# Eight slots for the gathered x1 rows, and drains instead of semaphores between an engine's own steps in the scatters' stage

## The reference

```python
# layer 0, 8 heads of 16: attention of every edge within the edges of one dst
Q = (x[src] @ Wq + bq);  K = (x[dst] @ Wk + bk);  V = (x[dst] @ Wv + bv)
scores = einsum('ehd,ehd->eh', Q, K) / 4 + edge_attr @ Wb + bb
alpha = segment_softmax(scores, dst)
x1 = layernorm(x + segment_sum(alpha * V, dst) @ Wo + bo)
# layer 1: one softmax over all edges
h = x1 @ W;  e = leaky_relu((h @ a1)[src] + (h @ a2)[dst])
out = layernorm(x1 + segment_sum(softmax(e)[:, None] * h[src], dst))
```

## Time and profile before

| | us |
|---|---|
| median of 3 runs (lowest, highest) | 1265.93 (1257.95, 1266.73) |
| the profiled execution, its own time | 1259.13 |
| its span, first to last instruction | 1257.4 |
| around the span | 1.7 |
| granted TensorE clock, mean over the span | 0.782 of 2.4 GHz |
| PE, DVE, ACT, POOL busy | 718.7, 759.0, 717.2, 764.1 |
| first gather of x to the last | 4.7 to 593 |
| first gather of x1 to the last | 639.5 to 937.8 |
| first scatter to the last | 954.6 to 1255.7 |

### The profile page before, as it was taken

One profiled execution on the slowest core, in us unless ns is written; L12 is line 12 of the kernel. 1 busy time (PEld: TensorE's weight loads), 2 busy tenths in 40 slices (PEclk: granted clock), 3 DMA queues, 4 the chain that ended last, 5 costly groups with the idle time before them and its releaser, 6 DMA issues.

```text
span 1257.4 us, 14313 instructions
## 1 busy us (share of the span) xinstructions
PE 718.7 (57%) x3271; PEld 482.5 (38%) x3271; DVE 759.0 (60%) x3537; ACT 717.2 (57%) x2048; POOL 764.1 (61%) x807
## 2 busy tenths in 40 slices
PE   0357767767667767676844564546455554544441
PEld 0235445445445544444634454545442211111110
DVE  4487767767777668677756555546437444444442
ACT  3457777777777777777713343424347554444443
POOL 7665666666666666665056665666654666666666
PEclk9888888787887888878967777767767766777775
DMA  7365565566665656654155767667755333433331
GB/s 211 110 187 158 184 209 168 178 188 214 203 200 200 203 161 193 197 166 163 68 171 162 216 207 221 198 211 223 208 172 163 121 113 115 119 116 120 107 107 46
DMA packets 89104, 209.87 MB, mean 167 GB/s; under 512 B 20602, under 2 KB 22793, under 8 KB 89008
## 3 DMA queue, kind: packets, MB, share of 16 engines
q1 hardware_dynamic: 63802, 161.20, 40.4%
q0 software_dynamic: 25216, 47.76, 13.6%
HBM read 122.85 MB, written 90.07 MB: 169 GB/s over the span
## 4 chain that ended last, share of the span: by engine, by line
another core or an unknown queue 19%; DVE 17%; ACT 13%; issue 8%; PE 5%; POOL 1%; DMA 1%; DVEq 0%; SPq 0%; POOLq 0%
ACT yb L801 3%; ACT node_out L801 2%; ACT src_b L952 2%; PE psum L748 2%; DVE src_b L1477 2%; DVE match L1152 2%; ACT xsT L961 2%; DVE nst L1492 1%; DVE nst L1254 1%; POOL out_dram L524 1%; DMA x1d_in<-x_all 1%; DVE shift L1485 1%; ACT h_res L965 1%; DVE node_in L1247 1%
## 5 line engine op out<-in xcount | busy, mean ns | idle before, releaser
L518 POOL DMA_INDIRECT xs<-in_x,src_tab x196 | 185.7, 947 | 153.0 <-remote 74.6
L524 POOL DMA_INDIRECT out_dram<-yb,at_last x196 | 194.7, 993 | 120.7 <-ACT yb L801 64.6
L518 POOL DMA_INDIRECT xs<-x_all,row_tab x196 | 187.5, 957 | 114.9 <-issue 55.8
L518 POOL DMA_INDIRECT h_res<-in_x,dst_tab x196 | 188.9, 964 | 59.8 <-issue 59.8
L801 ACT ACTIVATE h_res<-node_in,shift,rstd 128x128 f32<-128x128 f32 (+1 forms) x392 | 155.8, 482 | 0.3 <-DVE shift L1284 0.3
L776 PE MATMUL psum<-src_b,ident_inv 128*128 128x512 f32 x90 | 69.6, 865 | 132.8 <-DVE src_b L1477 111.7
L961 ACT ACTIVATE xsT<-psum 128x512 f32<-128x512 f32 x48 | 28.7, 597 | 200.0 <-remote 165.8
L606 PE MATMUL psum<-h_res 128*128 128x512 f32 x98 | 68.7, 789 | 120.9 <-ACT h_res L808 120.0
L748 PE MATMUL psum<-w,xsT 128*128 128x129 f32 x384 | 80.7, 376 | 91.8 <-ACT xsT L961 80.4
L748 PEld LDWEIGHTS psum<-w,xsT 128*128 128x128 f32 x384 | 71.6, 278 | 99.1 <-ACT xsT L961 86.6
L610 PE MATMUL psum<-xsT,h_res 128*128 128x512 f32 x98 | 85.2, 966 | 32.2 <-ACT xsT L812 19.4
(11 more groups left out here) (312 smaller groups left out, 1915.5 us busy)
## 6 DMA issues: line engine op xcount, KB each, us to landing
x1d_in<-x_all SPq DMA_DIRECT2D x98, 256.0 KB
node_in<-in_x SPq DMA_DIRECT2D x48, 512.0 KB
x_all<-h_res SPq DMA_DIRECT2D x48, 512.0 KB
out_dram<-node_out SPq DMA_DIRECT2D x48, 512.0 KB
x_all<-yb SPq DMA_DIRECT2D x49, 256.0 KB
src_b<-src_t SPq DMA_DIRECT2D x49, 256.0 KB
agg_rows<-src_b SPq DMA_DIRECT2D x49, 256.0 KB
node_in<-x_all SPq DMA_DIRECT2D x24, 512.0 KB
```

The source lines that it names most:

```text
L518: return pool.indirect_dma_start(out=to, out_offset=None, in_=table, in_offset=bass.IndirectOffsetOnAxis(ap=idx, axis=0))
L524: return pool.indirect_dma_start(out=table, out_offset=bass.IndirectOffsetOnAxis(ap=idx, axis=0), in_=rows, in_offset=None, bounds_check=l ...
```

## The change

Four things. (1) In the second stage the gathered rows have eight slots: the four of `xs`, and the four of `yb`, whose stored rows of the first stage are out by then. POOL's wait is for `x1_T` of g-8. (2) The semaphores that count landings are one for the first two tiles of a group and one for the last two, in both gather stages; who waits, waits for both. `xd`, with eight slots, has them per slot modulo 4. (3) Waits are added: POOL (before the first gather of x1) and SP (before it loads the late node chunks) wait until the last three node chunks are stored, and ACT, before each half of a late chunk, until it is loaded. (4) In the third stage DVE and ACT have a drain where they waited for a semaphore of their own; `r_chain` and `xa_done` count groups, from group 1 on; `e_stats` and `e_log` are gone. And DVE's order is another: the moments of group s-1 stand between the running sums of group s.

```diff
+    XG = XS + YB
+    PAIR = G // 2
...
+        def x1_rows(g):
+            u = g % XG
+            return xs[:, u, :] if u < XS else yb[:, u - XS, :]
+        def x1_landed(g):
+            u = g % XG
+            halves = (src_head, src_rest) if u < XS else (dst_head, dst_rest)
+            in_first_stage = len(range(u % XS, GROUPS, XS))
+            return [half[u % XS] for half in halves], 16 * PAIR * (in_first_stage + use(g, XG))
+        def nodes_landed(eng):
+            for k in range(GROUPS - NX, GROUPS):
+                eng.wait_ge(x1_stored[k % NX], landed(k, NX))
...
                 if s == GROUPS:
-                    for u in range(NX):
-                        pass
+                    nodes_landed(sp)
...
-            for u in range(NX):
-                pass
+            nodes_landed(pool)
...
-                wait(pool, x1_T, g - XS + 1)
+                wait(pool, x1_T, g - XG + 1)
                 for t, idx in enumerate(columns(row_tab, g)):
-                    gather(tile(xs[:, g % XS, :], t), x1_all, idx)\
-                        .then_inc(last_x1 if g == END and t == G - 1 else got_x1[g % XS], 16)
+                    gather(tile(x1_rows(g), t), x1_all, idx)\
+                        .then_inc(last_x1 if g == END and t == G - 1 else x1_landed(g)[0][t // PAIR], 16)
...
-                    pe.wait_ge(got_x1[s % XS], use(s, XS) * 16 * G)
+                    wait_x1(pe, s)
...
+                        act.wait_ge(late_loaded[j % NI], use(j, NI) * 16)
...
-                fn(logs[:, 0:G], nmv[:, s % 2, :, 1], ACT.Ln, bias=eps_cols[:, 0:1]).then_inc(e_log, 1)
-                act.wait_ge(e_log, s)
+                fn(logs[:, 0:G], nmv[:, s % 2, :, 1], ACT.Ln, bias=eps_cols[:, 0:1])
+                act.drain()
...
             def running(g, t):
-                dve.wait_ge(xa_done, g * G + (t if g == 0 else G - 1) + 1)
-                wait(dve, r_chain, g * G + t)
+                if g == 0:
+                    dve.wait_ge(xa_done, t + 1)
+                    wait(dve, r_chain, t)
+                else:
+                    if t == 0:
+                        dve.wait_ge(xa_done, summed(g))
+                    dve.drain()
...
             def aggregates(b):
-                dve.wait_ge(e_stats, b)
                 if b == 2:
                     dve.wait_ge(first_shift_done, G)
-                wait(dve, e_shift, b - 2)
                 wait(dve, e_rstd, b - 2)
+                dve.drain()
...
                 if edge(s):
-                    for t in range(1, G):
-                        running(s, t)
+                    running(s, 1)
                 if edge(s - 1):
-                    moments(s - 1)
+                    dve.wait_ge(e_y, s - 1)
+                    moments(s - 1, 0)
+                    if edge(s):
+                        running(s, 2)
+                    moments(s - 1, 1)
+                    if edge(s):
+                        running(s, 3)
+                    moments(s - 1, 2)
+                    moments(s - 1, 3)
                     aggregates(s - 1)
```

More of the change, by code:

```diff
@@ L291, in gnn_kernel @@
         agg_stored, part_got = sems("agg_stored", NA), sem("part_got")
-        e_y, e_stats, e_var, e_log, e_rstd, e_shift, e_applied = (
-            sem("e_y"), sem("e_stats"), sem("e_var"), sem("e_log"), sem("e_rstd"), sem("e_shift"), sem("e_applied"))
+        e_y, e_var, e_rstd, e_shift, e_applied = sem("e_y"), sem("e_var"), sem("e_rstd"), sem("e_shift"), sem("e_applied")
         e_scat = sems("e_scat", YB)
@@ L315, in last_bank, with wait_pairs, wait_x1 @@
             return 3 if t < G // 2 else 5
+        def x1_rows(g):
[6 more added lines that the diff above has]
+            return [half[u % XS] for half in halves], 16 * PAIR * (in_first_stage + use(g, XG))
+        def wait_pairs(eng, halves, g):
+            for half in halves:
+                eng.wait_ge(half[g % XS], 16 * PAIR * use(g, XS))
+        def wait_x1(eng, g):
+            halves, value = x1_landed(g)
+            for half in halves:
+                eng.wait_ge(half, value)
         def use(k, ring):
@@ L535, in _ @@
                 for t, idx in enumerate(columns(src_tab, g)):
-                    gather(tile(xs[:, g % XS, :], t), x, idx).then_inc(got_src[g % XS], 16)
+                    gather(tile(xs[:, g % XS, :], t), x, idx).then_inc((src_head if t < PAIR else src_rest)[g % XS], 16)
                 if g == 0:
@@ L539, in _ @@
                 for t, idx in enumerate(columns(dst_tab, g)):
-                    gather(tile(xd[:, g % XD, :], t), x, idx).then_inc(got_dst[g % XD], 16)
+                    gather(tile(xd[:, g % XD, :], t), x, idx).then_inc((dst_head if t < PAIR else dst_rest)[g % XS], 16)
             pool.wait_ge(fix_dve, 1)
@@ L778, in _ @@
                     for t in range(G):
[L779 removed]
+                        last = tr(bank[7][:, t * P:(t + 1) * P], tile(x1_rows(END), t), ident[:, :])
                     last
@@ L948, in weigh @@
             def weigh(g, tiles=range(G)):
-                wait(act, r_chain, (g - 1) * G)
+                if g >= 2:
+                    act.wait_ge(r_chain, summed(g - 2))
                 for t in tiles:
                     i = g * G + t
-                    fn(tile(xa[:, g % 2, :], t), h_res[:, i * DH:i * DH + D], ACT.Copy, scale=att[:, i:i + 1])\
-                        .then_inc(xa_done, 1)
+                    last = fn(tile(xa[:, g % 2, :], t), h_res[:, i * DH:i * DH + D], ACT.Copy, scale=att[:, i:i + 1])
+                    if g == 0:
+                        last.then_inc(xa_done, 1)
+                if g > 0 and tiles.stop == G:
+                    last.then_inc(xa_done, 1)
             for u in range(NO):
@@ L1503, in aggregates, with shift_of @@
                 last.then_inc(e_var, 1)
+            def shift_of(b):
+                dve.wait_ge(e_rstd, b)
+                if b == 2:
+                    dve.wait_ge(first_applied, G)
+                wait(dve, e_applied, b - 2)
+                v.scalar_tensor_tensor(shift[:, b % 2, 0:G], nmv[:, b % 2, :, 0], -1.0, rstd[:, b % 2, 0:G],
+                                       ALU.mult, ALU.mult).then_inc(e_shift, 1)
             def first_rows(t):
@@ L1528, in _ @@
                 i = END * G + t
-                last = v.tensor_tensor_reduce(out=dots[:, t * D:(t + 1) * D], in0=tile(xs[:, END % XS, :], t),
+                last = v.tensor_tensor_reduce(out=dots[:, t * D:(t + 1) * D], in0=tile(x1_rows(END), t),
                                               in1=v_src[:, :], scale=1.0, scalar=0.0, op0=ALU.mult, op1=ALU.add,
@@ L1573, in _ @@
             running(2, 1)
-            moments(1)
+            dve.wait_ge(e_y, 1)
+            for t in range(G):
+                moments(1, t)
             aggregates(1)
```

42 lines of the change are left out of this document (19 added, 23 removed).

## The result

| | before | after |
|---|---|---|
| median, same chip | 1263.51 us (1257.95 to 1266.73, 4 runs) | 1290.67 us (1288.16 to 1292.32, 4 runs) |
| ratio, 95% interval | | 1.0233 (1.0191 to 1.0274) |
| profiled span | 1257.4 | 1288.6 |
| first gather of x1 | 639.5 | 642.7 |
| gathers of x1, first to last end | 298.3 | 315.8 |

The change makes the kernel 2.3% slower, where 1231 us and a gain were forecast. The 31 us of the span are 3.2 ahead of the gathers of x1, 17.5 in their stage, 6.3 between the stages, 4.0 in the scatters' stage, and none behind it. More than half of the loss is in the stage where the forecast said "no change", and in the stage in which it said "-30" it is slower too.

The account below looks back on a forecast made before the run. It took POOL's row of indirect DMAs (gathers 298 us, scatters 301 us) as the bound; 1259.1 - 39.4 (drains) + 9 (order) + 0 (eight slots) + 3 (small waits) = 1231.7, stated as 1231 us, chance 0.38, range 1180 to 1290.

Parts of the forecast that it names:

- -30: Scatters' stage: the forecast gain, from -39.4 us for the drains and +9 us for DVE's new order.
- Who makes POOL pause: Last two stages: not the gathers' landing, but semaphores seen late while POOL issues indirect DMAs; pauses 52 and 48 us.
- Eight slots, "I take 0": x1 gathers' stage: a lead of two more groups is used up once, then POOL waits as before; 0 us.
- The +33 us: x1 gathers' stage: upper bound if POOL sleeps for `row_done` and wakes 1.5 us later in each of 22 pauses.
- rival 3: x1 gathers' stage: POOL's pause ended by `row_done`, slower, 1295 us; sign a stage over 320 us; chance 0.22.
- Drains, -39.4: Third stage: DVE's late look at its own semaphore goes, POOL's ten pauses shrink to 0.3 us; -39.4 us.
- rival 2: Third stage: the hold only moves on, ACT still idle 10 us a cycle before `logs`; 1262 us; chance 0.23.
- The order, +9: Third stage: two running sums behind `e_y` reach PE about 0.9 us later in each of 10 cycles; +9 us.
- Small waits, +3: Pairs' landing semaphores and waits for stored and loaded chunks: +2 us, set at +3 with SP's wait.

Follow-up runs that it names:

- pause_long: Kernel before with 24 small memsets on POOL behind each group of x1 gathers and of scatters: 1.0046 of the kernel before.
- pool_drain: Kernel before with a drain of POOL behind each group of four DMAs in the last two stages: 1.1567 of the kernel before.
- slots_alone: Changed kernel with eight slots and POOL's wait for g-8, but the third stage of the kernel before: 1.0177 of the kernel before.
- before_lead4: Kernel before (four slots) with LEAD 4 instead of 6: 1.0169 of the kernel before.
- before_again: Kernel before, unchanged, measured again under another name: 0.9974 of the kernel before.
- four_ahead_drains_old_order: Changed kernel, but POOL waits for the transposition of four groups before and all four running sums precede the moments; drains stay: 1.0042 of the kernel before.

## Why the prediction was wrong, point by point

*Who makes POOL pause: right.* PE did not wait for landing, and the semaphores are seen late while POOL issues without a gap. `pause_long` and `pool_drain` show it; this was the prediction's reading of the earlier trace rows, and I then did not carry it through. One size was off: of the ten waits before line 1502 nine took 3.8 to 5.9 us and one 0.7.

*Eight slots, "I take 0": this step failed.* It measured +1.8% in `slots_alone`, 22 us. I wrote that POOL would wait for the slower chain "as before, with longer runs and longer pauses", in other words that the idle time for one gather would stay. It does not, since the pause changes its kind. With four slots POOL stops with two finished index rows in hand (one at 4 of 23 pauses), and restarts when the held semaphores come through. With eight it stops only when it has none, and then the semaphore must come through *and* DVE must do its steps: 4.13 us for 2.52. The +33 us that I worked out as the other bound, 1.5 us for each of 22 pauses, had the right mechanism and place, and about the right size for one pause (3.7 us in 20 waits ended by `row_tab`, for 2.4 in the 22 "remote" ones). In sum it was too large: POOL's idle stretches of over 0.35 us behind the first gather add up to 77.9 us for 59.2, and the stage grew by 17.5 us, to 315.8, short of the 320 given as rival 3's sign. It was rival 3, with 0.22. That its 1295 us came within 5 is in part luck, since the other half is a gap to the first scatter 6.3 us longer, drains that cost something and a first stage 3.2 us longer. With `before_lead4` and `slots_alone` its condition "less than one group of indices in hand" is shown to be the cause, not merely present.

*Drains, -39.4: this step failed too.* I priced a drain like a satisfied wait, and forecast no idle time over 1 us before the aggregates; it was up to 3.47. A drain did not end with DVE's own steps: the moments in the rows above ended at 1100.22, the aggregates began at 1103.69. The drains' records are up to 4.1 us long, 55 of them over 1.3 us and 142.5 us together, and the 0.07 us that I took for a wait between two sums was read where POOL stood still. Net, drains cost 0.4% with four slots. A second part of the step is open to doubt too, that POOL's pause shrinks by as much as DVE's: where gaps ended the hold completely, the stage was at best 3 us shorter than that of `before_again`, and ACT waited for scatters to land instead. How much of that is the gaps' own price was not separated. The sentence of the Trainium skill ("VectorE: DVE Perf Modes", section "The DRAIN you can't avoid") that the semaphore "costs nothing extra" gave the better forecast here, no gain, though for a reason that it does not state: both forms meet the same hold. The bound "0, see rival 2" was there, and rival 2's sign, 10 us of ACT's idle time before `logs` in a cycle, came (112.4 us in all for 110.7). My drain's own cost of at most 0.1 us had no row under it.

*The order, +9: nothing measured* (1.0000 beside 1.0012, and 1.0052 beside 1.0042 with drains). The two sums behind `e_y` cost POOL nothing that shows; why stays open.

*Small waits, +3: 1.5 us (1.0012), with an interval that reaches to both sides of zero.* It agrees with +3, and with nothing.

*The range* ended at 1290, 0.7 us under the result. It was cut through the middle of the one rival that had a rule of its own for being slower, though both of its supports stood in the rows.

## What to carry to other kernels

Before a ring is deepened, find what the producer waits for next, and whether that comes by a longer way: a producer that stops while work is in stock restarts sooner than one that stops for want of work. Where a semaphore shows 4 to 6 us late, "remote", while GpSimd issues indirect DMAs without a gap, neither a drain nor a deeper buffer helped here. One gap after every four DMAs did, of some 1.2 us in the gathers' stage and 0.7 in the scatters', and it was worth its own time only where the rest of the chain then kept up: look first for the wait that will take the place of the one removed.

## What the runs showed of the hardware that I had not expected

- A drain of VectorE lasted from 19 ns to 4.1 us in the changed kernel and up to 6.1 us in `four_ahead_drains_old_order`; with gaps in GpSimd's DMAs, at most 0.98 us.
- A drain of GpSimd behind four indirect DMAs made the semaphores prompt (none of 48 over 0.12 us late) but GpSimd stood for up to 7.5 us.
- In the gathers' stage semaphores went from often held to mostly prompt between 18 and 20 memsets of 3 columns (17 and 3 of 48 late), at median gaps of 1.02 and 1.21 us between two groups of indirect DMAs. In the scatters' stage a gap of 0.70 us after four DMAs, or one of 0.97 us or more after eight, already left no stand of DVE over 0.64 us before its aggregates.
- Even 0.40 us of memsets after four scatters shortened their stage by 7 us: it halves the hold (DVE's stands before the aggregates 20.5 us for 41.5), and longer gaps that end it make ACT wait longer for scatters to land. Why shorter gaps are enough there than in the gathers' stage stays open. Nor do the runs show what the semaphores are held by, or whether an idle gap would do as well as one with memsets in it; neither was tried.
